# Three cross attentions in a twelve-layer perceiver kernel: a third buffer for packed keys, another order in the first step of the tail, dequantization and turning angles moved, the first weights in two parts

## The reference, cut to what matters

```python
q = split_heads(x_q @ Wq + bq) * dp_scale          # L0; L1 and L3 alike
k = split_heads(x_kv @ Wk + bk)
v = split_heads(x_kv @ Wv + bv)
attn = jax.nn.softmax(jnp.where(mask, neg, q @ k.T)) # L0 causal corner, L1 a key mask, L3 no mask
o = attn @ v;  return o @ Wo + bo
# L3 alone: the first two of the 16 dimensions of each head are turned by an angle, and mixed by a gate
q_rot = concat([cos_t*Q[..., :1] - sin_t*Q[..., 1:2], sin_t*Q[..., :1] + cos_t*Q[..., 1:2], Q[..., 2:]])
g = sigmoid(gate.mean());  scores = g * (q_rot @ K.T) + (1 - g) * (Q @ K.T)
# L0_ffn: weights rounded to 4 bits by blocks of 32 ("dequantization"), needed only after L0_attn
s = maximum(max(abs(wb), axis=-1) / 7, 1e-12);  wq = clip(round(wb / s), -8, 7) * s
# L2_xattn: random features over the whole context
rf_k = exp(K @ projection.T / 16);  KV = rf_k.T @ V;  out = rf_q @ KV / (rf_q @ sum(rf_k))
```

## Time and profile before

| | us |
|---|---|
| three runs | 1799.62, 1800.85, 1804.48 (median 1800.85) |
| the profiled execution | 1803.24 |
| its span, first to last instruction | 1801.4 |
| PE busy, PEld busy | 1596.9, 1386.4 |
| DVE, ACT, POOL busy | 1028.9, 935.6, 694.5 |
| mean granted clock | 0.927 |
| L0_xattn, L1_xattn, L3_xattn, from their first to their last instruction | 6.4 to 455.2, 537.7 to 1003.4, 1299.6 to 1741.4 |
| L2_xattn | 1143.3 to 1248.1 |

### The profile page before, as it was taken

How to read it: one execution, slowest core, us unless ns; L and a number is a source line. 1 busy time by engine, 2 the same in 40 slices (tenths; PEclk the granted TensorE clock), 3 DMA queues, 4 the chain that set the end, 5 groups by cost and what they waited for, 6 DMA issues and landing times. The chain is left out here.

```text
span 1801.4 us, 48551 instructions
## 1 busy us (share of the span) xinstructions
PE 1596.9 (89%) x19953; PEld 1386.4 (77%) x19959; DVE 1028.9 (57%) x1429; ACT 935.6 (52%) x1834; POOL 694.5 (39%) x618
## 2 busy tenths in 40 slices
PE   6999999998648999999999659898489999999965
PEld 5888888886537888888887549776368888888852
DVE  6666667776448777667773330001586666665622
ACT  4677767676123655555556213100157676767642
POOL 5655555540006555555540000000065555555202
PEclk9999999999668999999999869899599999999986
DMA  5665655543015665665554109484156555555440
GB/s 156 159 146 140 149 145 128 131 109 86 1 37 146 177 156 145 161 153 140 141 133 104 34 13 363 172 287 151 56 127 166 126 134 131 128 132 126 105 118 3
DMA packets 153853, 234.89 MB, mean 130 GB/s; under 512 B 24968, under 2 KB 71428, under 8 KB 152580
## 3 DMA queue, kind: packets, MB, share of 16 engines
q1 hardware_dynamic: 145698, 224.57, 47.2%
q10 hardware_dynamic: 7938, 7.23, 1.6%
HBM read 107.32 MB, written 0.23 MB: 60 GB/s over the span
## 5 line engine op out<-in xcount | busy, mean ns | idle before, releaser
L1278 DVE TENSOR_REDUCE L_xattn_maxima<-L_xattn_ps 128x4 f32<-128x1024 f32 x588 | 691.7, 1219 | 353.0 <-PE L_xattn_ps L841 351.1
L1018 ACT ACTIVATE L_xattn_p_ring<-L_xattn_ps 128x512 f32<-128x512 f32 x1176 | 676.5, 600 | 352.1 <-PE L_xattn_ps L890 350.6
L890 PE MATMUL L_xattn_ps<-L_xattn_q_packed,L_xattn_k_packed 128*128 128x256 f32 x2352 | 472.7, 304 | 8.5 <-DMA L_xattn_k_packed<-L_xattn_k_ring 6.0
L890 PEld LDWEIGHTS L_xattn_ps<-L_xattn_q_packed,L_xattn_k_packed 128*128 128x128 f32 x2352 | 344.4, 190 | 67.5 <-issue 29.3
L926 PE MATMUL L_xattn_ps<-L_xattn_p_ring,L_xattn_v_ring 128*17 128x128 f32 x9408 | 291.8, 275 | 1.0 <-ACT L_xattn_p_ring L1018 1.0
L809 PE MATMUL L_xattn_ps<-L_xattn_ctx_halves,L_xattn_w_halves 128*128 128x256 f32 x1764 | 262.7, 287 | 0.7 <-POOL L_xattn_ctx_halves L1165 0.6
L926 PEld LDWEIGHTS L_xattn_ps<-L_xattn_p_ring,L_xattn_v_ring 128*17 128x17 f32 x9408 | 244.5, 98 | 24.3 <-ACT L_xattn_p_ring L1018 1.6
L813 PE MATMUL L_xattn_ps<-L_xattn_w_halves,L_xattn_ctx_halves 128*128 128x256 f32 x1764 | 259.3, 285 | 0.3 <-ACT L_xattn_k_full L1031 0.3
L1180 POOL TENSOR_TENSOR L_xattn_k_ring<-L_xattn_k_full,consts 128x512 fp32r<-128x512 f32 x147 | 154.8, 1053 | 260.3 <-ACT L_xattn_k_full L1031 145.2
L809 PEld LDWEIGHTS L_xattn_ps<-L_xattn_ctx_halves,L_xattn_w_halves 128*128 128x128 f32 x1764 | 235.0, 194 | 4.0 <-issue 2.0
L813 PEld LDWEIGHTS L_xattn_ps<-L_xattn_w_halves,L_xattn_ctx_halves 128*128 128x128 f32 x1764 | 231.8, 192 | 2.9 <-ACT L_xattn_k_full L1031 0.7
(11 more groups left out here) (348 smaller groups left out, 1178.6 us busy)
## 6 DMA issues: line engine op xcount, KB each, us to landing
L_xattn_k_packed<-L_xattn_k_ring SPq DMA_DIRECT2D x588, 128.0 KB, 2.4
L_xattn_ctx_chunk<-in_ctx_chunks SPq DMA_DIRECT2D x147, 256.0 KB, 3.4
L_xattn_k_packed<-L_xattn_k_ring SPq DMA_DIRECT2D x588, 64.0 KB, 2.1
L_ffn_W<-in_experts_W SPq DMA_DIRECT2D x16, 1024.0 KB, 12.6
L_xattn_ctxT<-in_ctxT SPq DMA_DIRECT2D x14, 896.0 KB, 7.2
L_xattn_ctx<-in_ctx SPq DMA_DIRECT2D x14, 896.0 KB, 5.3
L_xattn_mask_chunk<-L_xattn_mask ACTq DMA_DIRECT2D x49, 128.0 KB, 3.1
weights<-in_pack_L_attn SPq DMA_DIRECT2D x46, 128.0 KB, 3.5
```

What stands on the lines that cost most here:

```text
L890: last = pe.matmul(L.ps[:, bank, d * 2 * S:(d + 1) * 2 * S], self.k_packed[s][:, quarter, d, half * P:(half + 1) * P], q[:, 2 * pair:2 * p ...
L1018: act.activation(self.p[t % P_RING][:, 4 * quarter:4 * quarter + 4, :], L.ps[:, E_BANK[unit], :].rearrange("p (h n) -> p h n", n=S), ACT.Exp)\
L1278: dve.tensor_reduce(out[:, 4 * v:4 * v + 4], L.ps[:, M_BANK + 2 * v:M_BANK + 2 * v + 2, :] .rearrange("p b (k n) -> p (b k) n", k=2), AX_X ...
```

## The change

`k_packed` gets a third buffer, and SP packs a chunk one step earlier; a fifth fill is waited for. In step 49 PE's second half attention, the turning and the batches change places, and step 50 has three banks. Dequantization runs from step 18, two operations per step. Parts of weights have 512 columns. The angles and factors of L3 move to L2_xattn (`TurnFactors`), with a DMA of their own for theta and gate, and the scale of the queries goes into the factors. The setup no longer waits; DVE makes the constants behind L0's queries. L0's weights come in two DMAs, `Wq, Wk, bq, bk` and the rest.

```diff
+FIRST_PART = 2 * DC * D + 2 * DC          # XATTN_PACK now: Wq, Wk, bq, bk, Wv, Wo, bv, bo
-PART = 256
+PART = 512
+    def load_first_weights(self, eng):
+        eng.dma_start(self.arena[:, at:at + FIRST_PART], ins[:, 0:FIRST_PART]).then_inc(self.loaded[0], 16)
+        eng.dma_start(self.arena[:, at + FIRST_PART:at + n], ins[:, FIRST_PART:n])\
+           .then_inc(self.second_part_loaded, 16)
-DEQUANTIZED_FROM = 35
+DEQUANTIZED_FROM = 18
-        free = E_BANKS if step < NCHUNK else E_BANKS + (KV_BANK,) if step == NCHUNK else TAIL_BANKS
+        free = E_BANKS if step < NCHUNK else E_BANKS + (KV_BANK,) if step < NCHUNK + 2 else TAIL_BANKS
-        self.k_packed = [sb(f"k_packed{c}", [P, 4, DC, KEYS], F32R) for c in range(2)]
+        self.k_packed = [sb(f"k_packed{c}", [P, 4, DC, KEYS], F32R) for c in range(3)]
# pack_keys; m % 3 likewise in load_key_mask, pe_unit, split_keys
-            sp.wait_ge(L["tails_filled"], 64)
-        if m >= 2:
-            sp.wait_ge(L["e_filled"], E_AT["scores", m - 2, 4 + quarter] + 1)
+            sp.wait_ge(L["tails_filled"], 80)
+        if m >= 3:
+            sp.wait_ge(L["e_filled"], E_AT["scores", m - 3, 4 + quarter] + 1)
# fill_tails: for c in range(3); sync:
-            m, b = step - LAG + 1, block_turned(step)
+            m, b = step - LAG + 2, block_turned(step)
# tensor, steps from NCHUNK on
                 self.pe_unit(pe, m, 1)
-                self.pe_batch(pe, step, 0)
                 self.pe_unit(pe, m, 2)
+                if step == NCHUNK:
+                    self.pe_attend(pe, m - 1, 0)
                 if b is not None:
                     self.pe_turned(pe, b)
                 self.pe_unit(pe, m, 3)
-                if step == NCHUNK:
-                    self.pe_attend(pe, m - 1, 0)
+                self.pe_batch(pe, step, 0)
                 self.pe_attend(pe, m - 1, 1)
                 self.pe_unit(pe, m, 4)
                 self.pe_unit(pe, m, 5)
-                self.pe_batch(pe, step, 1)
...
                 self.pe_attend(pe, m, 0)
+                self.pe_batch(pe, step, 1)
# scalar of CrossAttention: Exp, Sin, Exp of the turn removed (now TurnFactors.scalar, behind L2_xattn's loop)
# act_split_weights: for Wv in L0 act.wait_ge(self.net.second_part_loaded, 16)
# vector
-            self.turn_angles(dve, o)
-            self.turn_factors(dve, o)
-            for c in range(DC):
-                o.after(dve.tensor_scalar(self.qT_swapped[:, c, :], self.qT_swapped[:, c, :], tn[:, 20 + c:21 + c], ...
-                o.after(dve.scalar_tensor_tensor(self.qT[:, c, :], self.qT[:, c, :], tn[:, 22 + c:23 + c], ...
+            # turn_queries: four tensor_scalar from PSUM with the factors, one wait, one addition
+        o.after(dve.tensor_tensor(self.qT[:, :, :], self.qT[:, :, :], self.qT_swapped[:, :, :], ALU.add))
+        self.make_constants(dve)              # L0 alone, behind q_lo_ready
-                for i in range(2 if step < NCHUNK else 5):
+                for i in range(2):
# L2_xattn: sync starts with the DMA of "turn" (128 x 258 f32), vector:
+        self.turn.vector_angles(dve, o)       # 19 small operations, ahead of the long wait
         dve.wait_ge(L["chunk_summed"], self.CHUNKS + 3)
         dve.tensor_copy(self.kv[:, :], L.ps[0:self.M, 2, 0:D + 1]).then_inc(L["kv_ready"], 1)
+        self.turn.vector_factors(dve, o)      # 7 small operations, one behind the other
         dve.wait_ge(L["y_in_psum"], 1)
# setup: x first, then consts, load_first_weights, no wait; DVE's four constants moved to make_constants
```

More of the change, by code:

```diff
@@ L582, in __init__ @@
         self.causal, self.masked, self.turned = causal, masked, turned
+        self.first = L.name == LAYERS[0]
         self.norm = NormRows(L, bank=ACC_BANK)
@@ L687, in fill_tails @@
               .then_inc(L["tails_filled"], 16)
-        for c in range(2):
+        for c in range(3):
             sp.dma_start(self.k_packed[c][tail, :, :, :].rearrange("p q d t -> p (q d t)")
@@ L869, in pe_unit @@
             return
-        L, s, half, quarter = self.L, m % 2, u // 4, u % 4
+        L, s, half, quarter = self.L, m % 3, u // 4, u % 4
         unit = E_AT["scores", m, u]
@@ L931, in tensor @@
         L = self.L
+        self.wait_first(pe)
         self.norm.tensor(pe)
@@ L954, in tensor @@
                 self.pe_project(pe, step, 1)
+                if self.first:
+                    pe.wait_ge(L["constants_made"], 4)
                 self.pe_turned(pe, b)
@@ L999, in tensor @@
                 self.pe_attend(pe, m, 0)
+                self.pe_batch(pe, step, 1)
+        if self.first:
+            pe.wait_ge(self.net.second_part_loaded, 16)
         pe.wait_ge(L["sums_ready"], 1)
@@ L1061, in act_factor, with wait_first, make_constants @@
         act.activation(self.factor[:, :], L.ps[:, E_BANK[unit], :], ACT.Exp).then_inc(L["e_drained"], 1)
+    def wait_first(self, eng):
+        if self.first:
+            eng.wait_ge(self.net.first_loaded, 32)
+    def make_constants(self, dve):
+        L, net = self.L, self.net
+        if self.first:
+            identity = net.const("identity")
+            dve.tensor_copy(net.ident_bf[:, :], identity).then_inc(L["constants_made"], 1)
+            dve.tensor_tensor(net.spread[:, :, :], wide(identity[0:2 * H, 0:H], 32), wide(identity[0:2 * H, H:2 * H], 32),
+                              ALU.add).then_inc(L["constants_made"], 1)
+            dve.tensor_copy(net.causal_bf[:, :, :], times(net.const("causal"), 4)).then_inc(L["constants_made"], 1)
+            dve.tensor_copy(net.causal_T_bf[:, :, :], times(net.const("causal_T"), 4)).then_inc(L["constants_made"], 1)
     def act_split_weights(self, act):
@@ L1067, in act_split_weights @@
         for halves, name in zip(self.w_halves, ("Wk", "Wv")):
+            if self.first and name == "Wv":
+                act.wait_ge(self.net.second_part_loaded, 16)
             act.activation(halves[:, 0, :, :], self.w(name, c=DC), ACT.Copy).then_inc(L[f"{name}_hi_ready"], 1)
@@ L1097, in scalar @@
         L = self.L
-        if not self.turned:
-            act.activation(self.warm[:, 0:1], self.net.const("ones")[:, 0:1], ACT.Exp)
+        self.wait_first(act)
+        act.activation(self.warm[:, 0:1], self.net.const("ones")[:, 0:1], ACT.Exp)
         if not self.dequantizing:
@@ L1269, in reduce_batch @@
+        for c in range(DC):
+            last = dve.tensor_scalar(self.qT_swapped[:, c, :], L.ps[:, M_BANK, c * S:(c + 1) * S],
+                                     self.w("bq_swapped")[:, c:c + 1], tn[:, 20 + c:21 + c], ALU.add, ALU.mult)
+        o.after(last)
+        o.after(dve.tensor_tensor(self.qT[:, :, :], self.qT[:, :, :], self.qT_swapped[:, :, :], ALU.add))
     def reduce_batch(self, dve, step, d):
@@ L1387, in vector @@
                 self.update_shift(dve, o, b)
+        if self.first:
+            dve.wait_ge(net.second_part_loaded, 16)
         dve.wait_ge(L["tile_attended"], NT)
```

154 lines of the change are left out of this document (78 added, 76 removed).

## The result

Over twenty runs each the changed kernel has a median of 1796.56 us against 1801.41: ratio 0.9966, 95% interval 0.9954 to 0.9978. It is faster by 0.34%, about 6 us; 17 had been forecast. Its profiled execution spans 1795.3 us against 1801.4.

A forecast was written before the change was run, and what follows sets the result against it. PE was taken to set the time where never idle, so only tails, heads and L2_xattn's end count. Terms −8.1 −3.8 −3.1 −4.4 +0.7 +0 +1.3 = −17.4 gave 1783.5 us, range 1773 to 1795.

The forecast's parts named there:

- Tails, −15.0: Steps 49 to 55 and the last waits: −8.1 in L0, −3.8 in L1, −3.1 in L3.
- Dequantization hidden from step 18: L0's steady steps: dequantization from step 18 costs nothing while PE covers it; uncovered, some 36 us.
- L2_xattn, +1.3: L2_xattn: +0.85 at its end for seven chained operations, some 0.4 for its new first DMA.
- L3's head, −4.4: Start of L3: batch 0 comes 5.1 earlier, +0.7 given back; ends −3.0 and −6.5.
- SP now issues pack(1)'s eight DMAs ahead of the shift's load ...; I take +0.7 (0 to +3.1): L3's head, step 5: chunk 1's key DMAs (5 us) delay the shift's load, costing +0.7.
- L1's head: Start of L1: one more fill of 1.5, on context arriving before it is needed: 0, ends 0 and +1.5.
- L0's head, +0.7: Start of L0: batch 0 gains about 1, against one more fill and later context 5; ends −2.5 and +3.0.
- fifth fill 1.1 to 2.2: L0's head: chunk 0's pack waits for one fill more, each 1.1 to 2.2, with context 5 queued behind.
- ACT's wait for context 5: L0's head: the wait should be no shorter than 3.16 if the forecast is right.
- a first unit over 5 behind the shift's load: Heads: a first unit trailing the shift's load by over 5 would show the forecast wrong.
- (d): Rival: heads starve on SP's queue, PE stops and runs at half clock; +9.4, 1810, chance 0.04.
- The rule on the shared port: L3's head: DVE's addition and q_hi could wait for GpSimd's key splits, bringing the term to its smaller end, −3.0.

The follow-up runs named there:

- fill_ahead: Changed kernel with SP's list as before up to step 45, the one-step advance taken only in step 46, all five fills still in front: ratio 0.9908.
- late_deq: Changed kernel with dequantization from step 35 and five operations a step from step 49, as before the change: ratio 0.9978.
- late_pack: Changed kernel with three k_packed buffers but SP's list as before, a chunk's keys one step later in it: ratio 0.9952.
- shift_first: Changed kernel with the load of the first shift (step 5) ahead of chunk 1's eight key DMAs in SP's list: ratio 0.9974.
- after_again: The changed kernel itself, unaltered, measured a second time: 1796.65 us, ratio 0.9973.
- turn_in_L3: Changed kernel with angles, factors and the two changes of ACT's table back in L3's head: ratio 0.9964.
- late_fill: Changed kernel with only the fifth fill moved behind chunk 0's keys, SP's new order of packs kept: 1794.57 us, ratio 0.9957.
- factors_only: fill_ahead with ACT's turn operations ahead of L2_xattn's loop and the factors ahead of DVE's long wait: 1785.03 us, ratio 0.9912.
- old_setup: Changed kernel with the old setup: SP waits there, DVE makes constants ahead of L0_xattn, L0's weights come in one DMA: ratio 0.9956.
- old_order: Changed kernel with PE's order from step 49 on and the banks of step 50 as before: ratio 0.9947.
- context_first: Changed kernel with the advance only in step 46, fifth fill behind chunk 0's keys, context's load ahead of packed keys from step 6: ratio 0.9917.

## Why the prediction was wrong

- *Tails, −15.0:* −15.4, with the mechanism right and the sum partly by luck. L1 gave 2.6 in one trace and 4.9 in the other (3.8 forecast). Inside the tails the sizes were off: L0's steps 50 to 55 fell by 5.3 (5.4 forecast), L3's by 1.7 (2.5), since step 50's three banks cost 1.1 (5.4 long, before 4.3) instead of 0.2. What paid for it I hadn't counted: the clock stays up behind the tail, L3's output products take 1.14 instead of 2.07, and behind the last attention L0 and L3 gain 1.5 and 1.2 beyond the wait for the sums. The first of these rows is of before, the second of after:

```profile
1738.77 2.07 PE L273 MATMUL L_xattn_ps<-weights,L_xattn_ctx_chunk 128*128 128x256 f32 x4 [0.47 <-ACT L_xattn_ctx_chunk L261]
```
```profile
1733.35 1.14 PE L283 MATMUL L_xattn_ps<-weights,L_xattn_ctx_chunk 128*128 128x256 f32 x4 [0.47 <-ACT L_xattn_ctx_chunk L271]
```

- *Dequantization hidden from step 18:* right in the traces. L0 from chunk 6 to 48 takes 348.4 both before and in fill_ahead, and late_deq's tail is 5.3 longer.
- *L2_xattn, +1.3:* right in the part at its end (0.8). The stretch is 2.0 longer in both traces of the changed kernel, but only 1.0 and 1.2 in late_pack and shift_first, which have the same code there.
- *L3's head, −4.4:* the −5.1 at batch 0 was right (−5.5), but only 3.8 of it lasts to chunk 6 where the queue is in order (47.4 in fill_ahead): behind batch 0 PE now waits 1.51 and 0.54 for DVE's maxima. **The step that failed is "SP now issues pack(1)'s eight DMAs ahead of the shift's load ...; I take +0.7 (0 to +3.1)"**, counted in L3 only. It measured +3.2 in L3 (10.29 for 7.10; 10.23 in after_again), and the same place cost 1.5 and 2.5 in L0 and 3.3 and 1.3 in L1, where I had written 0. L1's share is the least certain: its waits for the load were 1.67 and 1.04, but late_pack and fill_ahead take 8.7 for that step without any such wait. In L0 another 1.65 followed at the second turning.

  Three things were missing. SP is already full there (in L3 it issues without a pause from 1325.57 on), so that the eight issues start only 1.1 ahead of the turning and last past it. They also stand ahead of the next context chunk, as shift_first shows. And the clock falls behind the stop in some heads: in L3 (2.05, 1.98) and in one L1 (1.67), in L0 behind 1.40 but not behind 1.31. L3's earlier batch 0 isn't the reason, as turn_in_L3 waits 1.99 with a late one.

  Taking the eight issues out of the heads gives 9.3 (fill_ahead against late_fill) and about 10 (factors_only against after_again), nearly the gap of 11: with them out, the ratio of 0.9908 is −16.6, beside the forecast −17.4. That the two come so close is partly luck, as fill_ahead's single terms differ from the forecast ones (L1's head +2.8 for 0, L3's −3.8 for −4.4, L0's −1.3 for +0.7).

  In the first pair of profiles (−6.1) the missing 11.3 are 3.9 in L3's head, 2.6 in L1's, 1.7 in L0 between chunks 6 and 48, 0.7 in L2_xattn, less 0.8 in the tails and L0's head; the other 3.2 lie in layers where single executions scatter by that much.
- *L0's head, +0.7; fifth fill 1.1 to 2.2:* +0.3, near by luck and wrong in kind. ACT's wait for context 5, named as a sign, fell from 3.16 to 1.90 (row below), and the fill makes no difference that shows in either pair. The loss sits at the two turnings. The other sign of being wrong, a first unit over 5 behind the shift's load, didn't appear (2.4 in L3): the load itself was late.

```profile
32.42 0.63 ACT L1111 ACTIVATE L_xattn_ctx_halves<-L_xattn_ctx_chunk 128x512 fp32r<-128x512 f32 x1 [1.90 <-DMA L_xattn_ctx_chunk<-in_ctx_chunks]
```

- *Rivals:* (d) named the place, the 3.1 and the clock's 1.7, but joined them to the fill and to tails at their smaller ends, and so got a chance of 0.04 as a slower kernel. The mechanism was real at about half its price. It belonged in the sum.
- *The rule on the shared port* was set aside as separated by no row. It fits the small operations at the second turning, and q_hi's two writes in L3, 3.20 together beside GpSimd's split where they took 2.36 before.

**Left open:** L1's head took either 40 to 41 or 43 us between chunks 0 and 6, in fill_ahead and factors_only with identical instructions; where the time goes is seen in part (next section), not what decides it. The values of the new setup and of the new order are below what these runs can tell.

## What to carry to other kernels

An instruction moved one step earlier in a queue is paid by everything behind it until the queue has slack again. Before moving DMAs in a list that serves several consumers, write down for each of them when the issuing engine would reach it, at the point where the queue is fullest, and take the advance where it is empty: here in step 46, not in the head. A wait of 1 to 2 on PE must be priced with the clock behind it, as a chance and not a certainty: here it fell behind some of them.

## What was not expected of the hardware

After a stop of 2.1 in L1's head PE runs at half clock for 3.4 us in the kernel before and for 10 in fill_ahead, both without an idle stretch behind it. Two windows of each, before first; their clocks are means, and by windows of 1 us the half clock ends near 583.8 and near 582.1:

```profile
580.00:584.00 4.00, 4.00 (x29) 3.44 (x29) 3.35 (x5) 0.27 (x1) 3.05 (x3) 0.57 0.27 77
584.00:591.00 7.00, 6.91 (x72) 6.23 (x74) 5.65 (x7) 4.47 (x9) 6.16 (x6) 1.00 0.85 204
```
```profile
571.90:576.00 4.10, 4.03 (x25) 3.56 (x24) 3.16 (x5) 0.27 (x1) 3.32 (x3) 0.50 0.44 144
576.00:584.00 8.00, 8.00 (x56) 7.21 (x56) 4.94 (x7) 3.02 (x6) 5.89 (x5) 0.61 0.88 218
```

It costs 3 us of L1's head. Of the 18 profiled executions ten have 42.8 to 43.5 between the drains of chunks 0 and 6, eight 39.7 to 40.9; the changed kernel has been seen in both groups, and so has the L1 of fill_ahead, which factors_only shares (43.3 and 39.8). The upper group has more than one cause. Six have the stretch of 10 (shift_first, late_pack, old_setup, old_order, fill_ahead, late_fill), late_deq has one of 13. The changed kernel and turn_in_L3 have two of 3.3, the second behind the wait for the shift's load, and context_first has none at this place, but 17 us at half clock further ahead in the same head (547 to 564), where fill_ahead has 7 (548 to 555). A single profile can't tell kernels apart by that much here. A VectorE operation of 0.17 on 16 columns can take 1.14 when GpSimd has just begun one. The kernel before has such ones too (1.06 at 76.02 in L0), at a place where PE doesn't wait for them.
